# Cross-attention kernel: row maxima turned by VectorE and DMA in place of TensorE's transposes, output projection issued five groups ahead

## What is computed

```python
n  = layernorm(x) * g1 + beta1                 # 4096 x 512
c  = layernorm(ctx) * g1 + beta1               # 3202 x 512
q, k, v = n @ Wq.T + bq, c @ Wk.T + bk, c @ Wv.T + bv      # 8 heads of 64
x1 = x + softmax(q k.T / 8) v @ Wo.T + bo
U  = ((layernorm(x1) * g2 + beta2) @ W_in.T + b_in) @ Bmat # 4096 x 64
s_t = silu(s_{t-1} @ A.T) + U_t                # a scan over the 4096 rows
out = x1 + s @ Cmat + (mean(ctxb) @ W_prog.T + b_prog)
```

## Time and profile before

| | |
|---|---|
| device time, median of 3 runs | 2356.67 us (2354.91 to 2357.35) |
| profiled execution, device time | 2354.21 us |
| profiled execution, span from first to last instruction | 2351.9 us |
| TensorE matmul busy | 2277.1 us, 97% |
| VectorE busy | 1732.7 us, 74% |
| GpSimd busy | 1583.7 us, 67% |
| ScalarE busy | 1121.4 us, 48% |
| mean granted TensorE clock | 0.981 |
| chain that ended last, TensorE's share | 83% |

### The profile page before, as it was taken

The page is one execution under the profiler, slowest core; times in us unless marked ns, Lnnn a source line. Parts: engine busy times, 40 slices in busy tenths (PEclk is TensorE's granted clock), DMA queues, the critical chain, the costliest instruction groups (busy, mean ns, idle before and its releaser), DMA issues.

```text
span 2351.9 us, 35969 instructions
## 1 busy us (share of the span) xinstructions
PE 2277.1 (97%) x14148; PEld 1321.2 (56%) x14148; DVE 1732.7 (74%) x2167; ACT 1121.4 (48%) x1429; POOL 1583.7 (67%) x1039
## 2 busy tenths in 40 slices
PE   8999989999999999999999999999999999998877
PEld 8998854555555545555555555555555555446653
DVE  5865546788888777888888887888887888646645
ACT  3654424454444444544454444544444445542354
POOL 1200026888888888888888889888888888884201
PEclk8999999999999999999999999999999999999987
DMA  6650225777677777776777777776777767877513
GB/s 241 217 177 10 81 74 120 155 155 156 155 154 160 172 164 171 174 159 153 164 158 178 165 174 170 155 155 154 156 157 159 155 154 162 188 174 220 171 45 143
DMA packets 158678, 365.01 MB, mean 155 GB/s; under 512 B 22511, under 2 KB 62063, under 8 KB 157870
## 3 DMA queue, kind: packets, MB, share of 16 engines
q0 software_dynamic: 59904, 218.13, 45.4%
q1 hardware_dynamic: 98606, 144.58, 19.0%
HBM read 95.41 MB, written 49.02 MB: 61 GB/s over the span
## 4 chain that ended last, share of the span: by engine, by line
PE 83%; POOL 4%; DMA 4%; issue 4%; DVE 3%; ACT 2%; SPq 0%; ACTq 0%; DVEq 0%; POOLq 0%
PE ps L1269 28%; PE ps L1142 10%; PE ps L1244 7%; PE ps L1246 7%; PE ps L1248 7%; PE ps L1106 4%; PE ps L1236 4%; DMA acca<-pt 3%; POOL accp L526 3%; PE ps L1124 3%; PE ps L1114 3%; PE ps L1333 2%; PE ps L1390 1%; PE ps L1087 1%; DVE mx_part L892 1%
## 5 line engine op out<-in xcount | busy, mean ns | idle before, releaser
L708 ACT ACTIVATE pt<-ps 128x1024 f32<-128x1024 f32 x800 | 779.1, 1021 | 909.3 <-PE ps L1248 886.1
L892 DVE TENSOR_REDUCE mx_part<-ps 128x2 f32<-128x1024 f32 x768 | 938.5, 1222 | 347.6 <-PE ps L1142 347.6
L526 POOL TENSOR_TENSOR accp<-accp,pt 128x1024 f32<-128x1024 f32 x416 | 1037.1, 2493 | 233.4 <-ACT pt L708 230.9
L1269 PE MATMUL ps<-pt,v 128*64 128x512 f32 x3328 | 805.9, 605 | 0.0
L965 DVE TENSOR_TENSOR ps<-ps,shb 128x1024 f32<-128x1024 f32 x403 | 493.2, 1224 | 51.8 <-PE ps L1248 51.8
L1269 PEld LDWEIGHTS ps<-pt,v 128*64 128x64 f32 x3328 | 202.2, 136 | 344.2 <-issue 336.4
L1142 PE MATMUL ps<-kk,qh 64*128 64x512 f32 x1536 | 350.0, 451 | 9.9 <-DVE mx_part L892 9.9
L1142 PEld LDWEIGHTS ps<-kk,qh 64*128 64x128 f32 x1536 | 143.5, 183 | 367.2 <-DVE mx_part L892 266.6
L1244 PE MATMUL ps<-qh,kk 64*128 64x512 f32 x1664 | 329.4, 391 | 4.9 <-ACT pt L708 4.9
L1248 PE MATMUL ps<-ql,kk 64*128 64x512 f32 x1664 | 329.7, 390 | 0.0
L1246 PE MATMUL ps<-qh,kk 64*128 64x512 f32 x1664 | 329.5, 391 | 0.0
(11 more groups left out here) (150 smaller groups left out, 1941.6 us busy)
## 6 DMA issues: line engine op xcount, KB each, us to landing
acca<-pt POOLq DMA_DIRECT2D x224, 512.0 KB, 4.9
accb<-pt POOLq DMA_DIRECT2D x160, 512.0 KB, 4.8
q_scratch<-kk SPq DMA_DIRECT2D x32, 512.0 KB, 4.4
acca<-accp POOLq DMA_DIRECT2D x32, 512.0 KB, 4.6
o_scratch<-ost SPq DMA_DIRECT2D x32, 512.0 KB, 3.1
og<-o_scratch SPq DMA_DIRECT2D x32, 512.0 KB, 5.8
shb<-m_scratch SPq DMA_DIRECT2D x31, 512.0 KB, 4.2
xs<-x SPq DMA_DIRECT2D x16, 512.0 KB, 6.5
```

The source lines that it names most:

```text
L526: nc.gpsimd.tensor_tensor(acc[:, :], acc[:, :], pt[n % PT_SLOTS][:, :], ALU.add).then_inc(added_p, 1)
L708: nc.scalar.activation(pt[n % PT_SLOTS][:, :], src, ACT.Exp, scale=SCALE).then_inc(exped, 1)
L892: nc.vector.tensor_reduce(mx_part[:, m % QT, :, m // QT], src, AX_X, ALU.max).then_inc(max_taken, 1)
L1269: ins = mm(ps[HD * h:HD * (h + 1), 6, :], v[:, t, f:f + HD], pt[n % PT_SLOTS][:, h * QB:(h + 1) * QB], start=(t == 0), stop=(t == NT - 1))
```

## The change

TensorE's transposes of the row maxima, ScalarE's copy and the waits that go with them are left only for the first unit. For units 1 to 31 VectorE reduces the partial maxima to `mx_row`, ordered by head and query tile, multiplies them by -1 into the first 8 columns of a zeroed 128 x 32 tile, and transposes that in blocks of 32 x 32 (`row_max`). SP sends the four blocks to DRAM in four DMAs, waits for them, and loads the row from DRAM into `sh` with a fifth; the broadcast into `shb` follows as before. TensorE waits for the load into `sh` at the start of a unit. In the output projection TensorE runs five groups ahead of its transposes, VectorE adds group 1 ahead of the first layernorm, scale and mean have six places in place of two, and the steps of unit 31's results move to other groups. The buffers for the attention output stay three.

```diff
 OG_SLOTS = 3
+AHEAD = 5
+LN_SLOTS = 6
...
-def turn_step(u):
...
-    return NJ - M_LEAD if u else NM * NJ // M_FIRST + 1
...
         mxp = at("mxp", [P, QT, HD + 1], RR + 11776)
+        mx_row = at("mx_row", [P, 2, QT], 2576)
+        shift_row = at("shift_row", [P, 32], 2624)
+        shift_col = at("shift_col", [P, 32], 2592, F32R)
         mx_part = at("mx_part", [P, QT, 2, 7], RR + 12040)
...
         yi = small[:, 18:20].bitcast(I32)
-        ya = small[:, 20:24].rearrange("p (s t) -> p s t", s=2)
+        ya = at("ya", [P, LN_SLOTS, GT], RR + 11776)
         yb = small[:, 24:26]
-        nmr = small[:, 26:30].rearrange("p (s t) -> p s t", s=2)
+        nmr = at("nmr", [P, LN_SLOTS, GT], RR + 11792)
         cu = [small[0:SD, 30:31], small[SD:2 * SD, 30:31]]
...
         max_turned = sem("max_turned"); shift_ready = sem("shift_ready")
-        scored = sem("scored"); sh_stored = sem("sh_stored"); shb_loaded = sem("shb_loaded")
+        scored = sem("scored"); sh_loaded = sem("sh_loaded"); shift_col_ready = sem("shift_col_ready"); sh_stored = sem("sh_stored"); shb_loaded = sem("shb_loaded")
         shifted = sem("shifted"); exped = sem("exped"); pv_done = sem("pv_done")
...
                 sp.wait_ge(shift_ready, w + 1)
-                sp.dma_start(m_scratch[w % 2], sh[w % 2][0:HD + 1:HD, :].bitcast(F32)).then_inc(sh_stored, 16)
-                sp.wait_ge(sh_stored, 16 * w)
+                rows = m_scratch[w % 2].rearrange("h (t b i) -> b (h t) i", b=4, i=32)
+                for b in range(4):
+                    sp.dma_start(rows[b], shift_row[32 * b:32 * b + 2 * QT, :]).then_inc(sh_stored, 16)
+                sp.wait_ge(sh_stored, 64 * w)
+                sp.dma_start(sh[w % 2][0:HD + 1:HD, :].bitcast(F32), m_scratch[w % 2]).then_inc(sh_loaded, 16)
                 wait(sp, shifted, tiles_added(w - 1))
...
                 load_x2(d)
-                if d == 6:
+                if d == 8:
                     fold_den(UNITS - 1)
...
                         sp.dma_start(at_sb[half * SD:(half + 1) * SD, :], a_t).then_inc(mod_loaded, 16)
-                if d == 9:
+                if d == 11:
                     spread_rden(UNITS - 1)
...
             ins.then_inc(ones_set, 1)
+            pool.wait_ge(k_stored, 32 * C_G)
+            nc.gpsimd.memset(shift_col[:, :].bitcast(F32), 0.0).then_inc(ones_set, 1)
...
                 add_bias(d)
-                if d == 10:
+                if d == 11:
                     scale_o(UNITS - 1)
-                if d == 12:
+                if d == 13:
                     low_o(UNITS - 1)
...
-            def shift(w):
-                act.wait_ge(max_turned, w + 1)
-                if w == 0:
-                    act.wait_ge(ones_set, 3)
-                nc.scalar.activation(sh[w % 2][0:HD + 1, :], ps[0:HD + 1, 7, :], ACT.Copy, scale=-1.0)\
-                    .then_inc(shift_ready, 1)
+            def first_shift():
+                act.wait_ge(max_turned, 1)
+                act.wait_ge(ones_set, 3)
+                nc.scalar.activation(sh[0][0:HD + 1, :],
+                                     ps[0:HD + 1, 7, :], ACT.Copy, scale=-1.0)                    .then_inc(shift_ready, 1)
...
-            shift(0)
+            first_shift()
             for u in range(UNITS):
...
                         high_o(u - 1)
-                    if j == turn_step(u) and u + 1 < UNITS:
-                        shift(u + 1)
                     if u == UNITS - 2 and j in (3, 5, 7, 9):
...
                     ins = nc.scalar.activation(xn[:, t], x1(d)[:, t], ACT.Identity,
-                                               bias=nmr[:, d % 2, t:t + 1], scale=ya[:, d % 2, t:t + 1])
+                                               bias=nmr[:, d % LN_SLOTS, t:t + 1], scale=ya[:, d % LN_SLOTS, t:t + 1])
                 ins.then_inc(normed2, 1)
...
                     take_den(UNITS - 1)
-                if d == 6:
+                if d == 5:
                     high_o(UNITS - 1)
...
+            def first_row_max():
+                dve.wait_ge(max_taken, NM)
+                nc.vector.tensor_reduce(mxp[:, :, 0:HD + 1:HD], mx_part[:, :, :, :], AX_X, ALU.max).then_inc(max_ready, 1)
...
                 dve.wait_ge(max_taken, NM * (w + 1))
-                wait(dve, max_turned, w)
-                nc.vector.tensor_reduce(mxp[:, :, 0:HD + 1:HD], mx_part[:, :, :, :], AX_X, ALU.max).then_inc(max_ready, 1)
...
+                if w == 1:
+                    dve.wait_ge(ones_set, 4)
+                wait(dve, sh_stored, 64 * (w - 1))
+                nc.vector.tensor_reduce(mx_row[:, :, :], mx_part[:, :, :, :].rearrange("p t h k -> p h t k"), AX_X, ALU.max).then_inc(max_ready, 1)
+                dve.wait_ge(max_ready, w + 1)
+                nc.vector.tensor_scalar(shift_col[:, 0:2 * QT], mx_row[:, :, :].rearrange("p h t -> p (h t)"), -1.0, None, ALU.mult)                    .then_inc(shift_col_ready, 1)
+                dve.wait_ge(shift_col_ready, w)
+                nc.vector.transpose(shift_row[:, :], shift_col[:, :].bitcast(F32)).then_inc(shift_ready, 1)
...
                 take_max(0, m, m)
-            row_max(0)
+            first_row_max()
...
-            def project(d):
+            def add_x(d):
                 dve.wait_ge(xb_ready, d + 1)
...
+            def norm2_scale(d):
                 dve.wait_ge(x1_ready, GT * (d + 1))
-                wait(dve, normed2, d - 1)
-                layernorm(d % 2, lambda t: x1(d)[:, t, :], ln2_ready)
...
+                wait(dve, normed2, d - LN_SLOTS + 1)
+                layernorm(d % LN_SLOTS, lambda t: x1(d)[:, t, :], ln2_ready)
...
+            add_x(0)
             for d in range(X_G):
-                project(d)
-                if d == 5:
+                if d == 0:
+                    add_x(1)
+                if d > 1:
+                    add_x(d)
+                norm2_scale(d)
+                if d == 7:
                     invert(UNITS - 1)
...
-            def turn_max(w):
...
-                pe.wait_ge(max_ready, w + 1)
-                wait(pe, den_taken, w - 1)
+            def first_turn():
...
+                pe.wait_ge(max_ready, 1)
                 for q in range(QT):
...
             pe.wait_ge(v_ready, GT * C_G)
-            turn_max(0)
+            first_turn()
             pe.wait_ge(ones_set, 2)
...
-                if t == 0:
-                    pe.wait_ge(shift_ready, u + 1)
+                if t == 0 and u == 0:
+                    pe.wait_ge(shift_ready, 1)
+                if t == 0 and u > 0:
+                    pe.wait_ge(sh_loaded, 16 * u)
                 for h, r in enumerate(rows):
...
                 pe.wait_ge(added_a[u % 2], 16 * (len(A_TILES) + 1) * (u // 2 + 1))
-                if u + 1 < UNITS:
-                    pe.wait_ge(shift_ready, u + 2)
+                wait(pe, den_taken, u)
                 for h in (0, 1):
...
                         score_tile(u, 2 * j + 1)
-                    if ahead and j == turn_step(u):
-                        turn_max(u + 1)
                     for w, m in todo[max(1, len(todo) - 1):]:
...
             pe.wait_ge(bo_ready, 1)
-            for d in range(OG_SLOTS):
+            for d in range(AHEAD):
                 project(d, 0)
...
             for d in range(X_G):
-                if d + OG_SLOTS < X_G:
-                    project(d + OG_SLOTS, 0)
+                if d + AHEAD < X_G:
+                    project(d + AHEAD, 0)
                 if d > 0 and d % 2 == 0:
                     finish(d // 2 - 1)
-                if d + OG_SLOTS < X_G:
-                    project(d + OG_SLOTS, 1)
+                if d + AHEAD < X_G:
+                    project(d + AHEAD, 1)
                 turn2(d)
...
                     spread_sum(UNITS - 1)
-                if d == 8:
+                if d == 6:
                     pe.wait_ge(cb_summed, 1)
...
                     mm(ps[0:SD, 7, 0:1], cb_sum[:, :], ones[:, 0:1], start=True, stop=True).then_inc(mean_mm, 1)
-                if d == 10:
+                if d == 8:
                     pe.wait_ge(mean_ready, 1)
```

## The result

The changed kernel takes 2362.97 us (median of 9 runs, 2360.38 to 2367.07); the kernel before, beside it, 2355.19 us (9 runs, 2353.88 to 2357.35). The ratio is 1.0033, with a 95% interval of 1.0023 to 1.0042: slower by 7.8 us, against a forecast of 2366.0 and a range of 2346 to 2384. The profiled execution of the changed kernel is the slowest of its nine, 2367.07 us with a span of 2365.1; the one of before took 2354.21.

The account below looks back on a forecast made before the run. TensorE was taken to bound attention. Attention's +10.0 us and the projection's +0.6, taken as 0, on the profiled 2354.21 gave 2364; with the runs' median 2.5 us higher, 2366, range 2346 to 2384.

Parts of the forecast that it names:

- The hold: In attention, VectorE's new SBUF-to-SBUF multiply waits until GpSimd's running addition ends: 2.1 us instead of 0.17.
- Transpose: VectorE's new 128 x 32 transpose in attention: 0.2 us, bounds 0.15 and 0.4, run when GpSimd's addition is over.
- Step 9: Attention step where TensorE's second piece waits for VectorE's reduction: 0.4 us longer than before, 5.3 us.
- How often: In attention, units 1 to 29 lose 0.4 us each, units 0 and 30 gain 0.80 each: +10.0 us.
- The DMA chain: SP's four stores and load into `sh` in each unit: 8 us of cover before TensorE needs it, no cost.
- The projection: Output projection after attention: its terms sum to +0.6 us, taken as 0, from -9 to +6.
- Head: Start of the output projection: TensorE's wait moves to project 3, some 7 us instead of 4.74, +2.4 us.
- Middle: Middle of the output projection: six places and more lead leave about 1 us of TensorE's waits, -10.9 us.
- Group 14: In the output projection, its load waits for a store 8 us later; 4 to 6 us of cover go, +4.5 us.
- Drain: End of the output projection: five groups instead of three transposed with no projection beside them, +5.6 us.
- Clock: In the output projection, TensorE's slow products after long waits: fewer such waits, but longer ones, -1 us.
- The rival with the lead: Multiply held as forecast in attention, but the output projection gains 9 us: 2358 us; chance 0.18.

Follow-up runs that it names:

- the late run: The changed kernel with multiply and transpose issued behind VectorE's first reduction of the next step: 2341.73 us, 0.9942 of the kernel before.

## Why the prediction was right

The sign, the size and the mechanism in attention came as forecast. The second half was forecast at 0 and measured at -4.5 us; that it came so near is partly luck, since terms that were wrong cancelled.

- **The hold** was the step on which all depended, and it was right: 2.08 us for a forecast of 2.1, ending with GpSimd's addition. The evidence had been a two-column multiply in another stage against a reciprocal of the right shape; the operation decides, not the shape. The run with the operand in PSUM adds what the rows could not say: the operation and the home of its source together.
- **Transpose** 0.211 us for 0.2, not held. **Step 9** 5.29 us for 5.3. TensorE's wait was 0.88 us, where I wrote some 1.2. The run without the multiply shows why: there TensorE starts its second piece 1202.40 - 1200.44 = 1.96 us behind the first, where the prediction had 2.63 - 0.80 = 1.83, and in the changed kernel it starts 1222.05 - 1219.06 = 2.99 behind, so it comes 1.03 us late. (The list's 0.88 counts from the end of the product before, and products follow each other a little before that end.) Of the 0.80 us of the transposes 0.67 come free at this point. The step's length isn't touched by that, since VectorE ends it. The whole attention stage agrees: from the second row maximum to the projection the run without the multiply takes 1721.21 us (377.67 to 2098.88) where before took 1741.76 (376.90 to 2118.66), 20.55 us for the 31 transposes, or 0.66 each, and not 24.8.
- **How often:** 29 waits for 29 units. The unit grew by 0.36 us for 0.4, so 29 x 0.36 = 10.4 us. Unit 0 gained 0.74 us for 0.80 (54.67 against 55.41 us from the second row maxima to the third, which holds its step with the transposes). The 0.80 of unit 30 didn't show: from the last row maxima to the projection it takes 73.24 us before (from 2045.42), 74.23 after (from 2060.05) and 74.24 without the multiply (from 2024.64), and why is open. The attention part alone measured +11.5 us (+7.8 to +15.1) for a sum of +10.0. In the changed kernel's own profile, its slowest run, the projection starts 15.6 us later. Of the rest over these terms 2.5 us lie ahead of the second row maxima (376.90 and 379.36), and the other 2.5 in six single units of 56.1 to 57.3 us, where before has one of 57.5.
- **The DMA chain** had its cover. I took 0.51 us for each store's issue; four took 1.38 together. From the end of the last issue to the load it was 3.2 us, where the 1.6 of the single store of before were taken. The way from the first issue to the load was thus 4.57 us and not 3.6; the two errors partly cancel. With the forecast's 0.33 and 3.9 us the load is there by 1229.7 (an estimate, since the trace gives no landing for it), and the next unit starts at 1236.80: some 7 us of cover for 8.
- **The projection** was forecast at 0 and measured at -4.5 us (-6.8 to -2.1). By terms:
  - Head: wait of 7.25 us at project 3 for a forecast of 7. Right.
  - Middle: 4.1 us in six waits, the longest of 1.92, where there were 14.4; -10.3 for -10.9. The size is partly luck. Of the 11.9 us for additions 3.7 are left, not the forecast 1, so they gave 8.2; the other 2.1 came from the waits for the small sums `cb_sum` and `mean` (2.25 and 0.21 before, 0.37 after), which the prediction had put at nothing. The run with the six places alone brings the additions' waits to 2.2 us with a lead of three.
  - **Group 14: wrong.** The prediction had its load 4.5 us late, from a store that goes 8 us later and products that come 1.6 us sooner, 9.6 us less room. TensorE's products of group 14 start with no wait for it:

```profile
2234.42 0.36 SPq L418 DMA_DIRECT2D o_scratch<-ost  x1
2237.22 0.91 SPq L423 DMA_DIRECT2D og<-o_scratch  x2
...
2244.74 5.74 PE L1350 MATMUL ps<-wo_hl,og 128*128 128x512 f32 x24
```

  Two things were off. From the store's issue to the products there were 2243.12 - 2226.20 = 16.9 us before and are 10.3 now: 6.6 us less room, not 9.6. And the prediction kept the 5.1 us of before from store to load, which came from one slow store: it took 5.0 us from issue to landing, where the median of all 32 stores of `ost` was 3.1 before and is 3.0 after. The new one landed in 2.7, so the load followed after 2.8, and its two parts landed in 3.5 and 4.7 us (3.9 and 5.8 before). From the store's issue to the last landing it took 11.3 us and takes 7.9. So 5.6 us of cover became 2.4 (16.9 - 11.3 and 10.3 - 7.9); by an estimate from these numbers, either error alone would still have left a wait of some 1 us.
  - **Drain: mis-sized.** +5.6 was forecast. The stretch grew by 13.0 us, of which 2 x (0.8 + 0.9) = 3.4 is work that left the middle, so 9.6. The missing 4.0 us: a pair of groups at the speeds of before took 2272.11 - 2262.31 = 9.80 us, which less the 3.4 is 6.4 and not 5.6; now the first pair takes 2273.14 - 2262.14 = 11.0 us, and the two stretches behind it are 1.0 us longer each than their like before. In these, the first transposes after each wait, which took 1.09 us, take 1.97, at a clock of 0.50 to 0.66 where it was 0.79 to 0.83. That the longer drain brings the low clock is not shown: the six places alone had 0.66, and the attention part alone 0.69, in drains of three groups. The 0.84 in the profile of before is the highest of the five profiles with a lead of three (the others have 0.66 to 0.70), and the prediction was built on it.
  - **Clock: mis-sized.** -1 was forecast for the rest of the stage. Head and middle had a granted clock of 0.89 over 29.71 us and 0.97 over 110.73 us; they have 0.92 over 43.00 and 1.00 over 81.65. What that costs is read from products at either speed, here those of before:

```profile
2118.66 11.17 PE L1333 MATMUL ps<-wo_hl,og 128*128 128x512 f32 x48
...
2225.31 7.33 PE L1333 MATMUL ps<-wo_hl,og 128*128 128x512 f32 x24 [0.41 <-DVE x_last L1008]
```

  Slow were 48 products in 13.97, 12 in 4.58 and 24 in 7.33, against 11.17, 3.0 and 5.7 at full speed: 6.0 us lost. After, only the 48 in 13.36 are slow, 2.2 us: -3.8. No slow spell is left in the middle.
  - Sum of the measured terms: 2.5 - 10.3 + 9.6 - 3.8 = -2.0, against -2.8 in the profiles. The remaining 0.8 us are not accounted for.

The rival with the lead (2358, its part -9) had the condition that the load of group 14 lands in time, and that came true. Its size did not: the -4.5 us measured lie half way between its -9 and the 0 that I took, since the -9 also wanted a cheap drain, and the drain cost 9.6 us where even I had 5.6. The range of 2346 to 2384 held the 2362.97.

## What to carry to other kernels

Before a VectorE operation is put on a path, look at what GpSimd does at that moment and where the operation's source lies: here a multiply of eight columns cost 2.1 us or 0.17, and 30 us of the kernel hung on it. The cures that cost nothing were to leave the sign to an operation that runs anyway, or to read the source from PSUM. A lead between two engines is worth what it hides, and each group of it is a group that is drained alone: with two, three, four and five groups the drains took 18.4, 21.0 to 23.1, 27.3 and 33.0 to 34.0 us. Here the number of places, not the lead, was what the pipeline lacked.

## What the runs showed of the hardware

- A multiply (TENSOR_SCALAR) of 128 x 8, SBUF to SBUF, issued inside a GpSimd addition, ends with that addition (2.098 us by the median of 31); issued outside one, it takes 0.160 us (median in the late run); with its source in PSUM it takes 0.167 us inside one. A transpose of 128 x 32 and a reduction of 56 to 8 columns, both SBUF to SBUF, take 0.21 us inside such an addition. The Trainium skill (SBUF — State Buffer, Who interferes with whom) says that tensor_scalar can take the port pair that GpSimd shares, that this is an exclusive lock, and that tensor_reduce never does. The trace agrees: the multiply inside an addition ends 0.02 to 0.04 us behind it, 31 times of 31, and the reduction takes its 0.21 us.
- VectorE's transpose of 128 x 32 in float32 took 0.211 us each time. The Trainium skill (VectorE: DVE Perf Modes, The three transpose paths) has 311 ns for 128 x 128 in 16 bits. No run here has that shape; for this one the measurement decides, and with the page's figure the sum would have been some 3 us too high.
- Four small stores in a row were issued in 1.38 us, 0.35 each, where a single one showed 0.51; the load that waits for them went out 3.2 us behind the last issue's end.
- In the drain TensorE's granted clock fell to 0.64 of its full 2.4 GHz, nearer to its lower level of 1.2 GHz, after stretches in which it was busy in short pieces between waits of 0.7 to 3.7 us; eight transposes took 1.97 us there, and 1.03 at 2258.76, right behind the last projection. With a lead of three the drain had 0.84 in the kernel before, 0.66 with the six places alone and 0.69 with the attention part alone.
